# Score keys from a transposed context instead of TensorE transposes, in a decoder layer

## The reference, cut to what matters

```python
xn = _layernorm(x, gamma_media, beta_media)          # 8 x 722 x 512 context
ln = _layernorm(latents, gamma_lat, beta_lat)        # 8 x 100 x 512
kv_input = jnp.concatenate([xn, ln], axis=1)         # 8 x 822 x 512
sim  = einsum('bhid,bhjd->bhij', q * DH**-0.5, k)    # 8 heads of 128
attn = softmax(sim);  out = einsum('bhij,bhjd->bhid', attn, v)
```

## Time and profile before

| | us |
|---|---|
| median of 3 runs (1093.06 to 1096.96) | 1093.59 |
| profiled execution, its own time | 1094.34 |
| its span, first to last instruction | 1092.1 |
| start to q phase | 0 to 98 |
| q phase (folded queries) | 98 to 164 |
| `rest` and 7 iterations | 164 to 673 |
| last batch | 673 to 722 |
| values, output, router | 722 to 820 |
| experts | 820 to 1092 |

### The profile page before, as it was taken

The page is one execution under the profiler, slowest core; times in us unless marked ns, Lnnn a source line. Parts: engine busy times, 40 slices in busy tenths (PEclk is TensorE's granted clock), DMA queues, the critical chain, the costliest instruction groups (busy, mean ns, idle before and its releaser), DMA issues.

```text
span 1092.1 us, 18662 instructions
## 1 busy us (share of the span) xinstructions
PE 1055.1 (97%) x6366; PEld 959.8 (88%) x6367; DVE 765.7 (70%) x1369; ACT 559.1 (51%) x1125; POOL 123.2 (11%) x108
## 2 busy tenths in 40 slices
PE   8999999999999999999999999999998999999996
PEld 7979889999999999999999999997976877788775
DVE  7987476948759488594884866674677956847981
ACT  4526454444443445434544455571555846737871
POOL 4422100000000000000000000000011311211331
PEclk9999999999999999999999999999999999999998
DMA  9242765032130320313204104377357974947961
GB/s 309 75 134 100 275 240 206 1 121 66 60 109 17 120 66 14 135 37 109 77 0 149 37 0 136 137 253 278 109 157 264 351 241 165 330 170 236 351 233 27
DMA packets 82181, 160.99 MB, mean 147 GB/s; under 512 B 12749, under 2 KB 29645, under 8 KB 80223
## 3 DMA queue, kind: packets, MB, share of 16 engines
q1 hardware_dynamic: 80382, 155.70, 41.6%
q0 software_dynamic: 1760, 4.79, 1.3%
HBM read 127.68 MB, written 33.78 MB: 148 GB/s over the span
## 4 chain that ended last, share of the span: by engine, by line
PE 71%; DVE 9%; DMA 8%; issue 5%; ACT 5%; POOL 1%; SPq 0%; DVEq 0%; POOLq 0%; ACTq 0%
PE bank L610 20%; PE bank L612 20%; PE bank L611 20%; DMA stage<-in_W 4%; PE bank L1088 3%; PE bank L1054 2%; DVE xn_l L1539 2%; DVE wsl L1539 2%; DMA gat<-scr_tokens,idc 2%; ACT wsh L1399 1%; PE bank L1106 1%; PE bank L1075 1%; PE bank L1073 1%; PE bank L1105 1%; DMA w<-in_WgT 1%
## 5 line engine op out<-in xcount | busy, mean ns | idle before, releaser
L610 PE MATMUL bank<-pt_h,xn_h 128*128 128x256 f32 (+1 forms) x576 | 170.4, 296 | 6.9 <-DVE pt_l L1539 6.9
L612 PE MATMUL bank<-pt_h,xn_l 128*128 128x256 f32 (+1 forms) x576 | 165.0, 286 | 0.0
L611 PE MATMUL bank<-pt_l,xn_h 128*128 128x256 f32 (+1 forms) x576 | 164.8, 286 | 0.0
L1539 DVE TENSOR_TENSOR wsl<-stage,wsh 128x2048 fp32r<-128x2048 f32 x64 | 145.7, 2289 | 24.7 <-ACT wsh L1399 22.7
L610 PE MATMUL bank<-xt_h,qt_h 128*128 128x410 f32 (+1 forms) x384 | 136.4, 355 | 3.5 <-ACT pr L1353 3.5
L1399 ACT CAST wsh<-stage 128x2048 fp32r<-128x2048 f32 x64 | 122.5, 1917 | 23.6 <-PE bank L612 12.1
L612 PE MATMUL bank<-xt_h,qt_l 128*128 128x410 f32 (+1 forms) x384 | 134.2, 349 | 0.0
L611 PE MATMUL bank<-xt_l,qt_h 128*128 128x410 f32 (+1 forms) x384 | 134.1, 349 | 0.0
L610 PEld LDWEIGHTS bank<-pt_h,xn_h 128*128 128x128 f32 x576 | 109.0, 189 | 9.5 <-issue 6.9
L1350 ACT ACTIVATE pr<-bank,smx 128x412 f32<-128x412 f32 x48 | 29.0, 605 | 161.2 <-DVE smx L1709 161.2
L611 PEld LDWEIGHTS bank<-pt_l,xn_h 128*128 128x128 f32 x576 | 109.2, 190 | 0.0
(11 more groups left out here) (253 smaller groups left out, 2476.5 us busy)
## 6 DMA issues: line engine op xcount, KB each, us to landing
stage<-in_W SPq DMA_DIRECT2D x64, 1024.0 KB, 7.0
scr_q<-st SPq DMA_DIRECT2D x16, 800.0 KB, 6.0
qf<-scr_q SPq DMA_DIRECT2D x8, 1600.0 KB, 6.9
zr<-scr_z SPq DMA_DIRECT2D x16, 800.0 KB, 6.0
scr_z<-zf SPq DMA_DIRECT2D x7, 1600.0 KB, 5.2
raw<-in_ctx SPq DMA_DIRECT2D x8, 768.0 KB, 4.7
raw<-in_ctx SPq DMA_DIRECT2D x8, 512.0 KB
wq<-in_Wq SPq DMA_DIRECT2D x1, 2048.0 KB, 18.3
```

The lines of the kernel that those rows point to most:

```text
L610: pe.matmul(dest, lh, rh, start=start and k == 0, stop=False)
L611: pe.matmul(dest, lh, rl, start=False, stop=False)
L612: last = pe.matmul(dest, ll, rh, start=False, stop=stop and k == n - 1)
L1539: return dve.tensor_tensor(dst, src, high.bitcast(F32), ALU.subtract)
```

## The change: what it does

The context is also handed over transposed (`ctxT`, features by rows). For each batch SP loads it into `rt`, 4 x 722 on 128 partitions. The statistics, which lie one row per partition, are written to DRAM as two rows of 768 (`store_stats`, four bytes a piece) and read back spread over all partitions (`load_stats`, `mrow`). A new event `R k` lets DVE subtract the mean and multiply by gamma and the inverse deviation, for feature block k. `T k` now has four events a batch: ACT adds beta and rounds to `xt_h`, DVE makes `xt_l`. PE has no share in `T`; event `D` goes. The 100 latent columns of `xt_h` and `xt_l` come by DMA from `d_lt`, where the already split latents (`xa_h`, `xa_l`) were written in the q phase. The order `plan` is new, `L` of batch 0 moves from the q phase into `rest`, and the load of the value weights (`wv`, whose place `mrow` now shares) moves from the end of the q phase behind the last `T`.

```diff
-    plan = [("S", 3), ("N", 2), ("PT", 1), ("S", 4), ("N", 3), ("B+", 0), ("Z", (0, 0)), ("PT", 2), ("N", 4), ("B+",
-            1), ("S", 5), ("L+", 0), ("Z", (0, 1)), ("PT", 3), ("Z", (0, 2)), ("L+", 1), ("Z", (0, 3)), ("S", 6),
-            ("Z", (1, 0)), ("T+", 0), ("Z", (1, 1)), ("N", 5), ("PT", 4), ("E", 6), ("Z", (1, 2)), ("N", 6), ("PT",
-            5), ("Q+", 0), ("Z", (1, 3)), ("PT", 6), ("Q+", 1), ("Q+", 2), ("Q+", 3), ("Z", (2, 0)), ("T+", 1),
-            ("T+", 2), ("Z", (2, 1)), ("T+", 3), ("T+", 4), ("Z", (2, 2)), ("T+", 5), ("T+", 6), ("Z", (2, 3)), ("D",
-            0), ("S+", 0), ("N+", 0), ("X+", 0), ("X+", 1), ("X+", 2), ("X+", 3), ("X+", 4), ("S+", 1), ("S+", 2),
-            ("N+", 1), ("X+", 5), ("PT+", 0), ("X+", 6)]
-    rest = [("X", k) for k in range(4)] + [("S", 0), ("X", 4), ("N", 0), ("X", 5), ("S", 1), ("X", 6), ("S", 2),
-                                           ("N", 1), ("PT", 0)]
+    plan = [("S", 3), ("N", 2), ("PT", 1), ("S", 4), ("B+", 0), ("PT", 2), ("N", 3), ("S", 5), ("N", 4), ("B+", 1),
+            ("Z", (0, 0)), ("PT", 3), ("N", 5), ("S", 6), ("Q+", 0), ("Q+", 1), ("Z", (0, 1)), ("Q+", 2), ("Q+", 3),
+            ("Z", (0, 2)), ("E", 6), ("Z", (0, 3)), ("N", 6), ("Z", (1, 0)), ("PT", 4), ("Z", (1, 1)), ("R+", 0), ("PT",
+            5), ("Z", (1, 2)), ("R+", 1), ("PT", 6), ("R+", 2), ("T+", 0), ("L+", 0), ("Z", (1, 3)), ("T+", 1), ("Z",
+            (2, 0)), ("R+", 3), ("Z", (2, 1)), ("T+", 2), ("T+", 3), ("Z", (2, 2)), ("L+", 1), ("Z", (2, 3)), ("S+", 0),
+            ("N+", 0), ("X+", 0), ("X+", 1), ("X+", 2), ("X+", 3), ("S+", 1), ("S+", 2), ("N+", 1), ("X+", 4), ("X+",
+            5), ("PT+", 0), ("X+", 6)]
+    rest = [("L", 0), ("X", 0), ("S", 0), ("X", 1), ("X", 2), ("N", 0), ("L", 1), ("S", 1), ("X", 3), ("X", 4), ("S", 2),
+            ("N", 1), ("X", 5), ("PT", 0), ("X", 6)]
...
+    early = {(1, 2 * k + 1): [("Q", k)] for k in range(ND)}
     for k in range(ND):
+        early[1, 2 * k] = [("T", k)]
...
+            def load_keys(b):
+                sp.dma_start(rt[:], a["ctxT"][b].rearrange("(c p) m -> p c m", p=P)).then_inc(s_rt, 16)
+            def store_stats(b):
+                for made, v, col in ((s_mvr, 0, mvr[:, :, 0]), (s_rsr, 1, rsr[:])):
+                    sp.wait_ge(made, b + 1)
+                    sp.dma_start(d_row[b, v].rearrange("(c p) -> p c", p=P), col, allow_slow_non_contiguous=True
+                                 ).then_inc(s_row, 16)
+            def load_stats(b, to):
+                sp.wait_ge(s_row, b * 32 + 32)
+                for v in range(2):
+                    sp.dma_start(to[:, v, 0:MEDIA], bc(d_row[b, v, 0:MEDIA], MEDIA)).then_inc(s_mrow, 16)
+            def load_latent_keys(b):
+                at = slice(b * T, (b + 1) * T) if isinstance(b, int) else bass.ds(b * T, T)
+                for v, to in enumerate((xt_h, xt_l)):
+                    sp.dma_start(to[:, :, MEDIA:KEYS].bitcast(F32), d_lt[v][:, :, at]).then_inc(s_ltin, 16)
+            def write_latent_keys(half):
+                cols = slice(half * HT, (half + 1) * HT)
+                sp.wait_ge(s_tel, (half + 1) * HALF)
+                for v, part in enumerate((xa_h, xa_l)):
+                    sp.dma_start(d_lt[v][:, :, cols], part[:, :, cols].bitcast(F32)).then_inc(s_ltout, 16)
...
                 if not half:
                     write_residuals(range(HALF, B))
+                    write_latent_keys(1)
+                    sp.wait_ge(s_lnout, 16 * B)
+                    sp.wait_ge(s_out_a, 16 * B)
+                    sp.wait_ge(s_tpl, B)
+                    sp.dma_start(rt0[:, :, 0:MEDIA], a["ctxT"][0].rearrange("(c p) m -> p c m", p=P)).then_inc(s_rt, 16)
+                    load_stats(0, mrow0)
+                    sp.wait_ge(s_ltout, 16 * 4)
+                    load_latent_keys(0)
...
+            def load_scores(b):
+                sp.wait_ge(s_ktl, b * ND)
+                load_keys(b)
+                store_stats(b)
+                load_stats(b, mrow)
+                sp.wait_ge(s_s, b * RT)
+                load_latent_keys(b)
...
             with sp.Fori(0, B - 2) as b:
+                load_scores(b + 1)
                 load_first(b + 2)
                 write_z(b)
...
+            load_scores(B - 1)
+            sp.wait_ge(s_ktl, B * ND)
+            sp.dma_start(wv[:], a["Wv"].rearrange("(c p) n -> p c n", p=P)).then_inc(s_wvd, 16)
...
# PE
-                        for c in range(ND):
-                            last = pe.transpose(t[:, c * P:c * P + r], raw[0:r, k, c * P:(c + 1) * P], ident[0:r, 0:r])
-                        last.then_inc(s_tb, 1)
-                    elif what == "S":
-                        if k == 0:
-                            tb.all_read(pe)
+                            pe.wait_ge(s_ktl, (b + 1) * ND)
+                            pe.wait_ge(s_ltin, (b + 1) * 32)
                             pe.wait_ge(s_qread, (b + 1) * 3 * ND)
# ACT
-                        act.copy(xt_h[:, :, c0:c0 + w], t[:].rearrange("p (c n) -> p c n", c=ND)[:, :, 0:w]
-                                 ).then_inc(s_hi, 1)
+                        first = isinstance(b, int) and b == 0
+                        act.wait_ge(s_nr, ND if first else b * ND + k + 1)
+                        act.activation(xt_h[:, k, 0:MEDIA], (rt0 if first else rt)[:, k, 0:MEDIA], ACT.Identity,
+                                       bias=gbm[:, 1, k:k + 1]).then_inc(s_hi, 1)
# DVE
+                    if what == "R":
+                        first = isinstance(b, int) and b == 0
+                        x, m = ((rt0, mrow0) if first else (rt, mrow))
+                        x = x[:, k, 0:MEDIA]
+                        if k == 0:
+                            dve.wait_ge(s_rt, b * 16 + 16)
+                            dve.wait_ge(s_mrow, b * 32 + 32)
+                        ch.add(dve.tensor_tensor(x, x, m[:, 0, 0:MEDIA], ALU.subtract))
+                        ch.join()
+                        dve.scalar_tensor_tensor(x, x, gbm[:, 0, k:k + 1], m[:, 1, 0:MEDIA], ALU.mult, ALU.mult
+                                                 ).then_inc(s_nr, 1)
+                    elif what == "T":
+                        x = (rt0 if isinstance(b, int) and b == 0 else rt)[:, k, 0:MEDIA]
                         high_part()
-                        c0, w = tcols(k)
-                        low(xt_l[:, :, c0:c0 + w], t[:].rearrange("p (c n) -> p c n", c=ND)[:, :, 0:w],
-                            xt_h[:, :, c0:c0 + w]).then_inc(read, 1)
+                        dve.scalar_tensor_tensor(xt_l[:, k, 0:MEDIA], x, gbm[:, 1, k:k + 1],
+                                                 xt_h[:, k, 0:MEDIA].bitcast(F32), ALU.add, ALU.subtract
+                                                 ).then_inc(s_ktl, 1)
...
                 if what == "q" and half:
                     low_queries(half, h)
-                    if h in (1, 4):
-                        rows_norm(0, h // 4)
+                    if h >= HALF:
+                        run(0, [("R", h - HALF)])
```

More of the change, by code:

```diff
@@ L231, in build @@
     qf = mem("qf", [P, HEADS, ND, T])
+    rt = mem.over(wv_h, "rt", [P, ND, MEDIA])
+    mrow = mem.over(wv, "mrow", [P, 2, MEDIA])
     base_b = base + 6 * ND * D * 4
@@ L235, in build @@
     xt_l = mem("xt_l", [P, ND, KEYS + 2], F32R)
+    rt0 = mem.over(xt_l, "rt0", [P, ND, KEYS + 2])
+    mrow0 = mem.over(xt_h, "mrow0", [P, ND, KEYS + 2])
     xn_h = mem("xn_h", [P, KC, D], F32R)
@@ L443, in bc @@
         return vec.rearrange("(o n) -> o n", o=1).broadcast_to([parts, n])
-    plan = [("S", 3), ("N", 2), ("PT", 1), ("S", 4), ("N", 3), ("B+", 0), ("Z", (0, 0)), ("PT", 2), ("N", 4), ("B+",
[6 rows of a table removed]
[L460 to L465, removed]
-    rest = [("X", k) for k in range(4)] + [("S", 0), ("X", 4), ("N", 0), ("X", 5), ("S", 1), ("X", 6), ("S", 2),
-                                           ("N", 1), ("PT", 0)]
-    assert sorted(rest) == sorted(e for e in first if e[0] not in "TQ")
-    TB0, HI0 = KC + 2, KC + ND + 2
-    TB_USES = KC + 2 * RT + 1
+    plan = [("S", 3), ("N", 2), ("PT", 1), ("S", 4), ("B+", 0), ("PT", 2), ("N", 3), ("S", 5), ("N", 4), ("B+", 1),
[6 rows of a table added]
+    rest = [("L", 0), ("X", 0), ("S", 0), ("X", 1), ("X", 2), ("N", 0), ("L", 1), ("S", 1), ("X", 3), ("X", 4), ("S", 2),
+            ("N", 1), ("X", 5), ("PT", 0), ("X", 6)]
+    after_rest = [(what[:-1], k) for what, k in plan if what in ("S+", "N+", "PT+", "X+", "L+")]
+    assert sorted(rest) == sorted(after_rest)
+    TB0, HI0 = 2, 2 * ND + 2
+    TB_USES = 2 * RT
     ZB_USES = 3 * ND
@@ L991, in latents, with project @@
                     last.then_inc(s_tpl, 1)
-            def project(half, u, run):
+            def project(half, u):
                 cols = slice(half * HT, (half + 1) * HT)
@@ L1014, in project @@
                         u += 1
-                    run(0, [e for e in early.get((half, h), []) if e[0] == "T"])
                     if not half and h >= HALF:
```

(16 more changed lines are left out.)

41 lines of the change are left out of this document (19 added, 22 removed).

## The result

The kernel after takes 1117.5 us (median of 4 runs, 1115.94 to 1119.51) against 1093.32 of the kernel before on the same chip: a ratio of 1.0215, 95% interval 1.0184 to 1.0246. It is slower by 2.1%; the forecast was 1073, range 1062 to 1087. The profiled execution has a span of 1117.3 us, 25.2 more than before.

What follows compares the result with a forecast made beforehand. PE was taken as the bound nearly everywhere. From 1094.34 us, loop -26.6, q phase -3.0 + 5.0, `rest` +4.9 and last batch -0.9 gave 1073.7; 1073 was predicted, range 1062 to 1087.

Steps and rivals of the forecast that it cites:

- the statistics' way through DRAM: Each loop iteration: two statistics stores and two spread loads take 8 us, between 6.8 and 16.0, and stay hidden.
- The budget: Loop: 10.5 us from POOL's end to `R 0` for the stores and loads; each microsecond over would cost PE seven.
- rival 2: Loop: statistics come late, `R 0` stands with `PT 5`, `PT 6` and `T` behind it; 1117 at 16.8 us; chance 0.11.
- The loop: Each iteration: transposes and two stalls give PE 4.4 us, new waits cost 0.6; net 3.8, over seven iterations -26.6.
- rival 4: Loop: the transposes cost nothing, because PE gives back their time as other waits; 1093; chance 0.05.
- rival 1: Loop's end: DVE paces it, 1 to 2 us more in `R`, `T` or waits; 1081 at 1.2; chance 0.23.
- rival 3: DVE in the loop: two SBUF sources halve its rate, eight new instructions take 0.75 us more; 1114; chance 0.02.
- The q phase: Ahead of the loop: seven transposes go, -3.0 us; PE stalls once because keys and statistics land late, +5.0.
- `rest`: Batch 0 after the q phase: `L 1` before `S 1` makes `S 3` start 4.1 us later; with `PT 2`'s wait, +4.9.
- The last batch: After the loop: the last batch loses its stall before `Z (2, 0)`, -0.9 us.

Runs made afterwards that it cites:

- Whole lines: Kernel after, but the loop's two stores write 128 pieces of 48 and 24 bytes, and `mrow` is loaded from batch 0's rows: 1077.21 us, 0.983.
- far pieces: Kernel after, but each loop store writes 128 four-byte pieces 512 bytes apart in DRAM, and `mrow` is loaded from batch 0's rows: 1078.80 us, 0.9861.
- New order: Kernel after with the four-byte stores and wait kept, but `B 1` ahead of `S 5`, `PT 5` ahead of `R 0`, `L` behind `T 3`: 1078.08 us, 0.9843.
- run with `R` later: New order with `L` back in the q phase, and batch 0's `R` and `T` there between the emptying of the banks: 1068.75 us, 0.9746.
- last kernel: As the run with `R` later, but `Q 0` to `Q 3` of batch 0 behind heads 3, 4, 6 and 7: 1065.9 us, 0.9747.
- run with few pieces: Kernel after, but each loop store writes 128 four-byte pieces side by side, and `mrow` is loaded from batch 0's rows: 1098.27 us, 1.0023.

## Why the prediction was wrong

**The step that failed** is the size of the statistics' way through DRAM: 8 us taken between bounds of 6.8 and 16.0, 14.3 measured. The budget was right (10.5 us; DVE was free 10.1 us after POOL's end), and rival 2 names what happened, in the right order: `R 0` late, `PT 5` behind it, `PT 6` on PE. The choice inside the bounds was made by the quiet queue and by the 768 pieces of the earlier trace rows in 2.1 us. But those pieces are read from DRAM into separate partitions; these are written to DRAM side by side. Whole lines and far pieces (1.4 to 1.5 us, plus some 4.3 for the loads and the time to issue them) give 6 to 7 us, the low end of the bounds. The price was wrong too. At one PE microsecond for each late one, 14.3 makes 3.8 x 7 = 27, about 1100. Measured are 5.7 us an iteration over 66: some 3.0 of standing still and 2.5 of low clock behind it, which the prediction had at nothing. That rival 2 names 1117 and 1117.5 was measured is luck: its 1117 belongs to a way of 16.8 us without the low clock and without the 8.1 us lost ahead of the loop.

**The loop** is otherwise as forecast. New order and whole lines give 65.79 us against the forecast of 66 (69.87 less 3.8): the change itself is worth 4.1 us an iteration. Line 1054 is gone, no wait stands before `Z (2, 0)`, `R` takes 0.91 and 0.97 us, `T`'s low part 0.97, DVE 56.3 an iteration. So the transposes' time was not given back as other waits (rival 4 is out), and DVE does not pace the loop's end (rival 1): in the new order it has the same work, and PE waits 0.4 us. The keys were asked for 29 us ahead (346.84 to 375.88), not 60; they were in time all the same, since `R 0` waited for `mrow`.

**Two SBUF sources** (rival 3): 0.97 us for 722 elements beside 747 ns for 512 is some 1.07 ns an element, near the 1.04 of the two-tensor instructions, where half the rate would be twice that. Rival 3 is out.

**The q phase** was taken as +2.0 with a stall of 5 us; the stall was 11.0. Keys and statistics came at 142.6 and not at 137: SP issued them at 131.24, after the residuals' landing, 5.9 us behind their last write, and `R 0` came 11.4 us later, with the latent columns on the same engines. The low clock behind the stall had no term. And the stall was not needed: it came from `R`'s place ahead of the banks, as the run with `R` later shows.

**`rest`** at +4.9 was right in kind and size: `S 3` waits 4.3 us, and taking `L` out gains 5.3. The last batch and the tail gained 2.2, 0.9 was forecast.

With the loss of the q phase and of `rest` (2.0 + 4.9) taken back, the forecast's own sum would be 1073.7 - 6.9 = 1066.8; the last kernel measures 1065.9. It is near by parts too: in its trace the loop gains 28.3 us (26.6 forecast), the part ahead of it loses 1.2, and the rest gains 2.5.

## What to carry to other kernels

When a value makes a round trip through memory and the trace shows no store of that shape, the price is the widest unknown of the sum: ask from which value on the gain is gone, and take the store that is most unlike a bulk copy at its upper bound, or change its shape. A wait put at the head of an in-order engine costs what stands behind it, and on PE the stall and the clock after it, so put behind it only what nobody needs soon. An order of work that gives a late transfer its time was as good here as a faster transfer.

## What the runs showed of the hardware

- Stores of four bytes side by side in DRAM: 768 take 9.0 to 9.65 us until the semaphore, 128 take 6.95, 128 of them 512 bytes apart 1.4, 128 lines of 24 bytes side by side 1.4. The DMA engines pass the pieces within about a microsecond (from 360 and from 362 in the kernel after); the rest of the time they stand at 0.00 until the landing is confirmed. Loads issued behind such stores crawl, on the same queue (15 GB/s) or another (20 to 47 GB/s). That small writes to one stretch of memory wait for one another fits all of this; no run looked inside. The Trainium skill's page "DMA: Bandwidth & Descriptors", section "Specifications", has pieces under 512 bytes read, modified and written: the pieces far apart show that this is not slow by itself.
- PE's granted clock fell from 2.4 to 1.2 GHz (0.50) behind each of the loop's seven stalls of 2.7 to 3.9 us in the kernel after, in the iteration shown from 378.5 to about 385; with products into an unread bank in the stall it stayed at 2.4. In the run with few pieces it fell behind stalls of 2.2 and 2.4 us and not behind those of 0.4 to 1.3.
